# Key features from stacked high and low halves of a head, with scatters and evictions moved, in a graph and attention kernel on one Trainium2 core

## The chip, the cores and the metric

The kernel runs on one core of one Trainium2 chip. The metric is the device time of one execution in microseconds (us), taken as the median of several runs. TensorE, VectorE (DVE), ScalarE (ACT), GpSimd (POOL) and SyncE (SP) each run their own list of instructions and meet at semaphores.

## What is computed

The reference is a network of two layers over 1024 nodes of 512 features, with 16384 weighted edges. Most of it is untouched by the change: a graph product by segment sums, a mixture of eight experts, a second graph layer, a linear attention and a small table of integer steps. The change is in the block with kernelized attention, which runs twice (DEPTH = 2) with 8 heads of 64 and 256 features a head:

```python
def softmax_kernel(data, proj, is_query, eps=0.0001):
    normalizer = d ** (-0.25)
    ratio = proj.shape[0] ** (-0.5)
    data_dash = jnp.einsum('bhnd,md->bhnm', data * normalizer, proj)
    diag = jnp.sum(data ** 2, axis=-1, keepdims=True) * 0.5 * normalizer ** 2
    if is_query:
        m = jnp.max(data_dash, axis=-1, keepdims=True)
    else:
        m = jnp.max(data_dash, axis=(-2, -1), keepdims=True)
    return ratio * (jnp.exp(data_dash - diag - m) + eps)

for i in range(DEPTH):
    y = layernorm(x, ln1_g[i], ln1_b[i])
    # q, k, v: y @ W + b, cut into 8 heads
    qp = softmax_kernel(q, proj[i], True)
    kp = softmax_kernel(k, proj[i], False)
    d_inv = 1.0 / jnp.einsum('bhnm,bhm->bhn', qp, kp.sum(axis=2))
    ctx = jnp.einsum('bhnm,bhnd->bhmd', kp, v)
    o = jnp.einsum('bhmd,bhnm,bhn->bhnd', ctx, qp, d_inv)
    x = x + o @ Wo[i] + bo[i]
    y = layernorm(x, ln2_g[i], ln2_b[i])
    x = x + gelu(y @ W1[i] + b1[i]) @ W2[i] + b2[i]
```

The tables of the second graph layer (edge weights and edge counts, 1024 x 1024 each) are built meanwhile, by adding the edges one column of 128 at a time into two tables in memory.

## The kernel before

**Jobs and banks.** All work of TensorE is cut into jobs, each of which fills one of the eight PSUM banks in turn. `job_plan` (line 100) lists the stages in their order with the engines that empty a bank: "A" is ScalarE, "D" VectorE, "AD" both. Job n uses bank n mod 8, and `open_job` (L633) lets TensorE start it only when job n-8 has been emptied. Each engine's own loop is written out in the same order, so what stands late in one engine's list is late for all jobs behind it.

**Weights.** Every 512 x 512 block of weights is loaded into one of two `raw` buffers and split into a high half by ScalarE (`split_hi`, L1201) and a low half by GpSimd (`lo`, L2272), both float32r, in one of three slots of `W`. A product with it takes three single-pass products of 512 columns: high by high, high by low, low by high (L649 to L651, `split_mm`). `slot_order` says which block follows which in the slots; `w_wait` lets TensorE wait for the low half.

**A layer.** Queries and keys come out transposed, 128 rows (two heads) by 512 nodes a job: `q_T` and `k_T`, float32, written by ScalarE with the bias. VectorE writes the values `V` and their sum (L1710 to L1718). While the keys are made, VectorE also prepares edges for the scatters (`edge_batch`, L1641 to L1662: six batches in layer 0) and adds the bias `bo` to `X` (L1700). Then four head pairs follow. In each, TensorE computes

- `kd`: eight tiles of key features, one float32 product of 512 columns each, `k_T` by the two heads' `proj` (L804),
- `qd`: the same for queries, eight tiles, in the midst of which `kt` (L810, the transposed maxima of the keys) and `kb` (L815) stand,
- `ctx` (L831), the transposes `eT` of the query exponentials (L822) and the output `o` (L845).

VectorE takes the maxima of each key tile (L1732), their maximum over the tiles (`kmaxp`, L1738), the query maxima (L1742), evicts the transposed exponentials (`E_T`, L1759), and for each output takes a reciprocal (`rden`, L1776) and a product (`o_mul`, L1779); the low halves of the output (`op_a`, L1725) come a pair later. ScalarE copies the features and takes the exponentials. After the pairs come `wo`, `up` and `down` in four blocks each (`wo0`, `up0.0`, `down0.0` and so on; the last number is the block).

**GpSimd.** It makes the low halves and, between them, issues the scatters (`scatter`, L2334): for each column of 128 edges one indirect DMA into `table_w` and one into `table_c` (L2348), each of which waits for the last one into the same table. There are 128 pairs. How many stand between which low halves is written out in the loop.

```python
for name in ("wq", "wk", "wv"):
    if name != "wq":
        lo(f"{name}{l}")
    if l:
        scatter({"wq": 4, "wk": 6, "wv": 13}[name])
for hp, name in enumerate((f"wo{l}", f"up{l}.0")):
    if l == 0:
        scatter(10)
        pool.wait_ge(kdiag_ready, hp + 1)
    lo(name)
    if l:
        scatter(12)
scatter(12 if l else 4)
lo(f"down{l}.0")
```

## Time and profile before

| | |
|---|---|
| median of 3 runs | 1808.42 us (1804.3 to 1811.17) |
| the profiled execution, its time | 1808.56 us |
| its span | 1806.5 us |
| TensorE busy | 1676.0 us, 93% |
| VectorE busy | 1064.4 us, 59% |
| ScalarE busy | 695.4 us, 38% |
| GpSimd busy | 992.6 us, 55% |
| granted TensorE clock, mean | 0.97 of full speed |

The profile is one execution on the chip. A row of a timeline gives the start, the duration, the engine, the line of the kernel, the operation with the tiles that it writes and reads, their shapes, the number of instructions that were put into the row, and in brackets the idle time just before them with what ended it. A granted clock of 1.00 is 2.4 GHz, 0.50 is 1.2 GHz. Times in rows count from the start of the span. A float32 matmul leaves two records.

### The profile page before, as it was taken

How to read it: one execution, taken by the hardware profiler on the slowest of the kernel's cores; microseconds unless marked ns; L12 is line 12 of the kernel's file. 1: busy time of each engine (PE TensorE's matmuls, PEld its weight loads, DVE VectorE, ACT ScalarE, POOL GpSimd, SP SyncE). 2: the span in 40 equal slices, each digit the busy share in tenths (PEclk: the TensorE clock that was granted, in tenths of full speed). 3: DMA queues.
4: the chain of work that ended last, by engine and by line, in shares of the span. 5: the costliest groups of instructions: out<-in, count | busy, mean ns of one | idle time of the engine just before them, and what ended most of it. 6: DMA issues, size and time to landing. Idle time of an engine off the chain costs nothing.

```text
span 1806.5 us, 19998 instructions
## 1 busy us (share of the span) xinstructions
PE 1676.0 (93%) x7799; PEld 1302.2 (72%) x7799; DVE 1064.4 (59%) x1809; ACT 695.4 (38%) x916; POOL 992.6 (55%) x534
## 2 busy tenths in 40 slices
PE   6999999999989999999996999999999489999986
PEld 6766568788765457788875878777878478887863
DVE  7677878999936877543266442333333475432385
ACT  4535345333533443333412555556565221211112
POOL 4348412467777878588623666766676452333312
PEclk9999999999989999999996999999999799999998
DMA  9652102545422222322334878777775601121001
GB/s 342 172 161 24 24 1 73 128 120 108 103 27 24 1 24 1 93 48 47 99 129 168 292 249 272 247 262 246 269 248 180 198 8 57 60 70 55 16 0 47
DMA packets 146509, 212.05 MB, mean 117 GB/s; under 512 B 43724, under 2 KB 60336, under 8 KB 145168
## 3 DMA queue, kind: packets, MB, share of 16 engines
q1 hardware_dynamic: 98464, 176.96, 29.9%
q0 software_dynamic: 42832, 18.84, 8.5%
q10 hardware_dynamic: 5120, 14.99, 2.5%
q8 instruction: 62, 1.02, 0.2%
q14 instruction: 31, 0.25, 0.0%
HBM read 186.69 MB, written 30.08 MB: 120 GB/s over the span
## 4 chain that ended last, share of the span: by engine, by line
PE 73%; DVE 14%; POOL 4%; ACT 3%; issue 3%; DMA 3%; DVEq 0%; POOLq 0%
PE PS L649 19%; PE PS L651 18%; PE PS L650 18%; PE PS L804 5%; PE PS L831 3%; PE PS L845 3%; PE PS L822 2%; POOL table_c L2348 1%; POOL table_w L2348 1%; PE PS L692 1%; PE PS L986 1%; DVE h_op L1994 1%; DMA hg_dram<-hg 1%; DVE kmax L1732 1%; DVE picked L1648 1%
## 5 line engine op out<-in xcount | busy, mean ns | idle before, releaser
L2272 POOL TENSOR_TENSOR W<-raw,W 128x2048 fp32r<-128x2048 f32 x40 | 193.3, 4834 | 306.6 <-ACT W L1201 306.6
L2348 POOL DMA_INDIRECT table_w<-edge_add,edge_ix x128 | 204.2, 1595 | 109.2 <-DMA table_w<-edge_add,edge_ix 75.9
L2348 POOL DMA_INDIRECT table_c<-edge_add,edge_ix x128 | 206.4, 1613 | 59.5 <-issue 35.4
L649 PE MATMUL PS<-op_b,W 128*128 128x512 f32 x576 | 227.0, 394 | 6.6 <-DVE op_b L1628 3.3
L650 PE MATMUL PS<-op_b,W 128*128 128x512 f32 x576 | 225.4, 391 | 0.0
L651 PE MATMUL PS<-op_b,W 128*128 128x512 f32 x576 | 225.4, 391 | 0.0
L649 PE MATMUL PS<-W,op_a 128*128 128x512 f32 x480 | 187.8, 391 | 5.1 <-DVE op_a L1800 1.8
L651 PE MATMUL PS<-W,op_a 128*128 128x512 f32 x480 | 186.9, 389 | 0.0
L650 PE MATMUL PS<-W,op_a 128*128 128x512 f32 x480 | 186.8, 389 | 0.0
L2391 POOL TENSOR_TENSOR W<-raw,W 128x2048 fp32r<-128x2048 f32 x30 | 143.4, 4791 | 44.9 <-ACT W L1436 44.9
L1201 ACT ACTIVATE W<-raw 128x2048 fp32r<-128x2048 f32 x40 | 76.6, 1922 | 163.1 <-PE PS L651 104.9
L649 PEld LDWEIGHTS PS<-op_b,W 128*128 128x128 f32 x576 | 108.9, 189 | 32.0 <-DVE op_b L1628 3.8
L651 PEld LDWEIGHTS PS<-op_b,W 128*128 128x128 f32 x576 | 108.8, 189 | 23.0
L650 PEld LDWEIGHTS PS<-op_b,W 128*128 128x128 f32 x576 | 109.0, 189 | 22.3
L1370 ACT ACTIVATE G<-PS,colv 128x512 f32<-128x512 f32 x64 | 44.2, 691 | 179.6 <-PE PS L651 178.1
L649 PEld LDWEIGHTS PS<-W,op_a 128*128 128x128 f32 x480 | 90.1, 188 | 25.7 <-issue 3.2
L649 PE MATMUL PS<-W,x_op 128*128 128x512 f32 x248 | 98.7, 398 | 6.3 <-DVE x_op L1984 4.8
L651 PEld LDWEIGHTS PS<-W,op_a 128*128 128x128 f32 x480 | 90.1, 188 | 18.9
L650 PEld LDWEIGHTS PS<-W,op_a 128*128 128x128 f32 x480 | 90.1, 188 | 18.4
L1984 DVE TENSOR_TENSOR x_op<-PS,x_op 128x512 fp32r<-128x512 f32 x21 | 13.9, 688 | 145.6 <-ACT x_op L1443 145.6
L1800 DVE TENSOR_TENSOR op_a<-G,op_a 128x512 fp32r<-128x512 f32 x64 | 63.5, 1014 | 58.9 <-ACT op_a L1371 58.6
L1436 ACT ACTIVATE W<-raw 128x2048 fp32r<-128x2048 f32 x46 | 88.0, 1914 | 24.8 <-DMA raw<-in_L_ffn_w_dram 15.2
(426 smaller groups left out, 3774.7 us busy)
## 6 DMA issues: line engine op xcount, KB each, us to landing
raw<-in_L_ffn_w_dram SPq DMA_DIRECT2D x46, 1024.0 KB, 6.0
...
```

What stands on the lines that cost most here:

```text
L649: pe.matmul(ps, lhs_hi, rhs_hi, start=start, stop=False)
L650: pe.matmul(ps, lhs_hi, rhs_lo, start=False, stop=False)
L651: return pe.matmul(ps, lhs_lo, rhs_hi, start=False, stop=stop)
L804: pe.matmul(bank(n), feat[:, hp, t * P:(t + 1) * P], proj[:, :, :].rearrange("p a m -> p (a m)"), start=True, stop=True).then_inc(job_full, 1)
L831: mm = pe.matmul(bank(n)[:, (2 * h + mh) * VW:(2 * h + mh + 1) * VW], kd[:, h, t, mh * P:(mh + 1) * P], V[:, t, 2 * hp + h, :], start=(t = ...
L845: mm = pe.matmul(bank(n)[h * DH:(h + 1) * DH, :], ctx_sb[:, part, 2 * h + mh, :], E_T[:, 2 * h + mh, c * HALF:(c + 1) * HALF], start=(mh = ...
L1201: act.activation(W[:, s % SLOTS, 0, :], raw[:, raw_no[name] % 2, :], ACT.Copy).then_inc(hi_done, 1)
L1436: act.activation(ring_w[b % RING][:, 0, :], ring_raw[b % RING], ACT.Copy).then_inc(block_hi, 1)
L1800: dve.tensor_tensor(op_a[:, 1, at], G[:, j, :], op_a[:, 0, at].bitcast(F32), ALU.subtract).then_inc(hidden, 1)
L2272: pool.tensor_tensor(lo_at, raw[:, r % 2, :], hi_at.bitcast(F32), ALU.subtract).then_inc(lo_done, 1)
L2348: pool.indirect_dma_start(out=tb, out_offset=bass.IndirectOffsetOnAxis(ap=edge_ix[:, i, c:c + 1].bitcast(U32), axis=0), in_=edge_add[:, i, ...
L2391: pool.tensor_tensor(ring_w[b % RING][:, 1, :], ring_raw[b % RING], ring_w[b % RING][:, 0, :].bitcast(F32), ALU.subtract)\
```

## The change

**Keys.** `k_T` is replaced by two float32r stacks. `k_A` holds, in partitions 0 to 63, the high half of a pair's first head, and in 64 to 127 its low half; `k_B` holds the second head's low half in 0 to 63 and its high half in 64 to 127. ScalarE writes the high halves (two activations of 64 partitions in place of one of 128), VectorE the low halves (`key_lo`: two operations a key job, each reading PSUM and the high half in 64 partitions and writing the other 64). `proj_k` holds the projection's high and low half for both heads. A key tile becomes four float32r products of 256 columns: for each head, its stack by `proj_k`'s high and by its low half.

**Order.** The projection's transposes move from the end of the stage before into the key stage, behind key job 4. The last two edge batches move between the key jobs' low halves, and the `bo` additions behind them. The odd `E_T` evictions go to ScalarE. `k_B` lies in slot 1 of `W` and `rden` in slot 0, so `up{l}.0` takes slot 1 ahead of `wo{l}`'s slot 2, its high half is made after the last pair's query exponentials, and its low half after `wo`'s and all scatters up to there. GpSimd's scatters around `wv1`, `wo1` and `up1.0` are dealt out anew; their number stays.

```diff
@@ -102,19 +102,20 @@
...
     stages = [("xn_T", 4, "AD"), ("gnn_w_T", 4, "AD"), ("hg", 2, "A"), ("xn_T", 4, "AD"), ("par_T", 1, "D"), ("hg", 4, "A"),
-              ("y_T0", 4, "AD"), ("hg", 2, "A"), ("y_T0", 4, "AD"), ("edge_T", 1, "D"), ("proj0", 1, "A")]
+              ("y_T0", 4, "AD"), ("hg", 2, "A"), ("y_T0", 4, "AD"), ("edge_T", 1, "D")]
     for l in range(DEPTH):
...
             stages.append((f"q{l}", 8, "A"))
-        stages += [(f"k{l}", 1, "A"), (f"rq{l}", 2, "A"), (f"k{l}", 2, "A"), (f"dq{l}", 1, "A"), (f"k{l}", 5, "A"),
+        stages += [(f"k{l}", 1, "AD"), (f"rq{l}", 2, "A"), (f"k{l}", 2, "AD"), (f"dq{l}", 1, "A"), (f"k{l}", 2, "AD"),
+                   (f"proj{l}", 1, "AD"), (f"k{l}", 3, "AD"),
                    (f"v{l}", 1, "D"), (f"rk{l}", 2, "A"), (f"v{l}", 1, "D"), (f"dk{l}", 1, "A"), (f"v{l}", 6, "D"), (f"vsum{l}", 1, "A")]
...
             stages += [("kd" + s, 8, "AD"), ("qd" + s, 2, "A"), ("kt" + s, 1, "D"), ("qd" + s, 2, "A"),
-                       ("kb" + s, 1, "D"), ("qd" + s, 4, "A"), ("ctx" + s, 1, "D"), ("eT" + s, 8, "D"),
-                       ("o" + s, 4, "D")]
+                       ("kb" + s, 1, "D"), ("qd" + s, 4, "A"), ("ctx" + s, 1, "D")]
+            stages += [("eT" + s, 1, "A" if t % 2 else "D") for t in range(NT)] + [("o" + s, 4, "D")]
         stages += [(f"wo{l}", 6, "D"), (f"y2_T{l}", 4, "AD"), (f"wo{l}", 2, "D"),
@@ -122,7 +123,7 @@
...
             else:
-                stages += [(f"proj{l + 1}", 1, "A"), (f"down{l}.{fb}", 6, "D"), (f"y_T{l + 1}", 4, "AD"), (f"down{l}.{fb}", 2, "D")]
+                stages += [(f"down{l}.{fb}", 6, "D"), (f"y_T{l + 1}", 4, "AD"), (f"down{l}.{fb}", 2, "D")]
     stages += [("gnn", 6, "D"), ("xt_T", 4, "AD"), ("gnn", 2, "D"), ("gate_T", 1, "A"), ("xt_T", 4, "AD"), ("gate_T", 1, "A"), ("gate", 1, "D"),
@@ -229,8 +230,8 @@
...
     for l in range(DEPTH):
-        slot_order += [f"wq{l}", f"wk{l}", f"wv{l}", f"wo{l}"]
-        for fb in range(MLP):
+        slot_order += [f"wq{l}", f"wk{l}", f"wv{l}", f"up{l}.0", f"wo{l}", f"down{l}.0"]
+        for fb in range(1, MLP):
             slot_order += [f"up{l}.{fb}", f"down{l}.{fb}"]
@@ -280,7 +281,7 @@
...
         q_T = place("q_T", [P, NK, N], F32, at_a)
-        k_T = place("k_T", [P, NK, N], F32, at_a + 4 * 4096)
+        k_A = place("k_A", [P, NK, N], F32R, at_a + 4 * 4096)
         x_pair = place("x_pair", [P, NT, 2, D], F32R, at_b)
@@ -292,6 +293,7 @@
...
         W = place("W", [P, SLOTS, 2, BLK], F32R, at_w)
+        k_B = place("k_B", [P, NK, N], F32R, at_w + 4 * 2 * BLK)
         hg = place("hg", [P, NT, D], F32, at_w + 4 * 2 * 2 * BLK)
@@ -302,7 +304,8 @@
...
         o_mul = place("o_mul", [P, 2, HALF], F32, at_e)
-        rden = place("rden", [P, 2, HALF], F32, at_e + 4096)
+        rden = place("rden", [P, 2, HALF], F32, at_w)
+        proj_k = place("proj_k", [P, 2, NBF], F32R, at_e + 6144)
         tmp = place("tmp", [P, 4, D], F32, at_e)
@@ -768,7 +771,6 @@
...
 
-            projection_job(0)
             for l in range(DEPTH):
@@ -783,6 +785,8 @@
...
                             head_columns("q", l)
+                        if i == 1 and j == 4:
+                            projection_job(l)
                 w_wait(f"wv{l}")
@@ -797,12 +801,22 @@
...
                     s = f"{l}.{hp}"
-                    for x, feat in (("kd", k_T), ("qd", q_T)):
+                    if hp == 0:
+                        evacuated(f"proj{l}", 1)
+                        evacuated(f"k{l}", 8)
+                    for x in ("kd", "qd"):
                         for t in range(NT):
...
                             open_job(n)
-                            pe.matmul(bank(n), feat[:, hp, t * P:(t + 1) * P], proj[:, :, :].rearrange("p a m -> p (a m)"),
-                                      start=True, stop=True).then_inc(job_full, 1)
+                            mine = slice(t * P, (t + 1) * P)
+                            if x == "kd":
+                                for h, stack in enumerate((k_A, k_B)):
+                                    for i in range(2):
+                                        mm = pe.matmul(bank(n)[:, h * NBF:(h + 1) * NBF], stack[:, hp, mine], proj_k[:, i, :],
+                                                       start=(i == 0), stop=(i == 1))
+                            else:
+                                mm = pe.matmul(bank(n), q_T[:, hp, mine], proj[:, :, :].rearrange("p a m -> p (a m)"), start=True, stop=True)
+                            mm.then_inc(job_full, 1)
                             if x == "qd" and t == 1:
@@ -836,6 +850,7 @@
...
                     for c in range(2):
+                        evacuated("eT" + s, 4 * c + 3)
                         evacuated("eT" + s, 4 * c + 4)
@@ -862,8 +877,6 @@
...
                         feature_job(JOB_AT[f"up{l}.{fb}", j], op_b, slot_of[f"up{l}.{fb}"] % SLOTS, j % 4, j // 4)
-                    if fb + 1 == MLP and l + 1 < DEPTH:
-                        projection_job(l + 1)
                     w_wait(f"down{l}.{fb}")
@@ -1253,7 +1266,8 @@
...
                 act.activation(proj[0:DH, 0, :], bank(n)[0:DH, 0:NBF], ACT.Copy, scale=NORMALIZER)
-                act.activation(proj[DH:P, 1, :], bank(n)[DH:P, 0:NBF], ACT.Copy, scale=NORMALIZER).then_inc(job_act, 1)
+                act.activation(proj[DH:P, 1, :], bank(n)[DH:P, 0:NBF], ACT.Copy, scale=NORMALIZER)
+                act.activation(proj_k[:, 0, :], bank(n)[:, 0:NBF], ACT.Copy, scale=NORMALIZER).then_inc(job_act, 1)
 
@@ -1273,7 +1287,6 @@
...
             hi_half("y_T0", op_b, 1, ln_gb(0, 0), True)
-            projection_out(0)
             split_hi("wk0")
@@ -1291,22 +1304,29 @@
...
             for l in range(DEPTH):
-                for i, (x, dst) in enumerate((("q", q_T), ("k", k_T))):
+                for i, x in enumerate(("q", "k")):
                     for j in range(8):
...
                         m, c = j % 4, j // 4
+                        b = 8 + 4 * i + m
+                        cols = slice(c * HALF, (c + 1) * HALF)
                         if i == 0 and l and j == 2:
...
                             act.wait_ge(job_full, JOB_AT[f"rq{l}", j // 4] + 1)
-                        act.activation(G[:, j, :], bank(n), ACT.Square, bias=colv[:, l, 8 + 4 * i + m:9 + 4 * i + m]).then_inc(squared, 1)
-                        act.activation(dst[:, m, c * HALF:(c + 1) * HALF], bank(n), ACT.Identity,
-                                       bias=colv[:, l, 8 + 4 * i + m:9 + 4 * i + m]).then_inc(job_act, 1)
+                        act.activation(G[:, j, :], bank(n), ACT.Square, bias=colv[:, l, b:b + 1]).then_inc(squared, 1)
+                        if i == 0:
+                            act.activation(q_T[:, m, cols], bank(n), ACT.Identity, bias=colv[:, l, b:b + 1]).then_inc(job_act, 1)
+                        else:
+                            act.activation(k_A[0:DH, m, cols], bank(n)[0:DH, :], ACT.Identity, bias=colv[0:DH, l, b:b + 1])
+                            act.activation(k_B[DH:P, m, cols], bank(n)[DH:P, :], ACT.Identity, bias=colv[DH:P, l, b:b + 1]).then_inc(job_act, 1)
                         if i == 1 and j == 0:
...
                             columns_out("q", 0, l)
+                        if i == 1 and j == 4:
+                            projection_out(l)
                         if i == 0 and l and j == 2:
@@ -1314,7 +1334,6 @@
...
                 split_hi(f"wo{l}")
-                split_hi(f"up{l}.0")
                 if l == 0:
@@ -1354,6 +1373,13 @@
...
                         query_exp(t)
+                    if hp == HEADS // 2 - 1:
+                        split_hi(f"up{l}.0")
+                    for t in range(1, NT, 2):
+                        n = JOB_AT["eT" + s, t]
+                        act.wait_ge(job_full, n + 1)
+                        act.activation(E_T[:, :, t * P:(t + 1) * P], bank(n).rearrange("p (q n) -> p q n", q=4), ACT.Identity,
+                                       bias=eps_ones[:, 0:1]).then_inc(job_act, 1)
                 o_to_hi(HEADS // 2 - 1)
@@ -1375,7 +1401,6 @@
...
                     split_hi(f"wq{l + 1}")
-                    projection_out(l + 1)
                     for i in range(3):
@@ -1693,8 +1718,30 @@
...
                     dve.wait_ge(job_done, DONES[n])
-                for b in range(EARLY_BATCHES) if l == 0 else range(LATE_BATCH, EC // EB):
+                def key_lo(j):
+
+                    n = JOB_AT[f"k{l}", j]
+                    m, cols = j % 4, slice(j // 4 * HALF, (j // 4 + 1) * HALF)
+                    dve.wait_ge(job_act, ACTS[n])
+                    dve.scalar_tensor_tensor(out=k_A[DH:P, m, cols], in0=bank(n)[0:DH, :], scalar=colv[0:DH, l, 12 + m:13 + m],
+                                             in1=k_A[0:DH, m, cols].bitcast(F32), op0=ALU.add, op1=ALU.subtract)
+                    dve.scalar_tensor_tensor(out=k_B[0:DH, m, cols], in0=bank(n)[DH:P, :], scalar=colv[DH:P, l, 12 + m:13 + m],
+                                             in1=k_B[DH:P, m, cols].bitcast(F32), op0=ALU.add, op1=ALU.subtract).then_inc(job_done, 1)
+
+                first, past = (0, EARLY_BATCHES) if l == 0 else (LATE_BATCH, EC // EB)
+                for b in range(first, past - 2):
                     edge_batch(b)
+                for j in range(8):
+                    key_lo(j)
+                    if j == 1:
+                        edge_batch(past - 2)
+                    elif j == 3:
+                        edge_batch(past - 1)
+                    elif j == 4:
+                        n = JOB[f"proj{l}"]
+                        dve.wait_ge(job_act, ACTS[n])
+                        dve.scalar_tensor_tensor(out=proj_k[:, 1, :], in0=bank(n)[:, 0:NBF], scalar=NORMALIZER,
+                                                 in1=proj_k[:, 0, :].bitcast(F32), op0=ALU.mult, op1=ALU.subtract).then_inc(job_done, 1)
                 row_wait(f"bo{l}")
@@ -1768,7 +1815,7 @@
...
                     ins.then_inc(job_done, 1)
-                    for t in range(NT):
+                    for t in range(0, NT, 2):
                         e_t(t)
@@ -2354,15 +2401,13 @@
...
                     if l:
-                        scatter({"wq": 4, "wk": 6, "wv": 13}[name])
-                for hp, name in enumerate((f"wo{l}", f"up{l}.0")):
-                    if l == 0:
-                        scatter(10)
-                        pool.wait_ge(kdiag_ready, hp + 1)
-                    lo(name)
-                    if l:
-                        scatter(12)
-                scatter(12 if l else 4)
+                        scatter({"wq": 4, "wk": 2, "wv": 17}[name])
+                if l == 0:
+                    scatter(10)
+                    pool.wait_ge(kdiag_ready, 1)
+                lo(f"wo{l}")
+                scatter(36 if l else 14)
+                lo(f"up{l}.0")
                 lo(f"down{l}.0")
```

VectorE in the key stage of layer 0, before: behind the last edge batch (`edge_ix`) come the `bo` additions to `X` and then the values.

```order
L1652 TENSOR_REDUCE edge_add<-picked 128x2x4
L1656 TENSOR_SCALAR batch<-edge_add 128x8
L1658 SCALAR_TENSOR_TENSOR batch<-keycols,trash,batch 128x8 x2
L1662 TENSOR_SCALAR edge_ix<-batch,trash 128x8 x2
L1700 TENSOR_TENSOR X<-X,rowv 128x512 x8
L1710 COPY V<-dexp 128x64
L1711 TENSOR_TENSOR G<-PS,rowv 128x512
```

The same place in the changed kernel, from the end of the last batch: four more pairs of low halves of keys (four pairs stand ahead, around the batches) and the projection's low half.

```order
L1687 TENSOR_SCALAR edge_ix<-batch,trash 128x8 x2
L1726 SCALAR_TENSOR_TENSOR k_A<-PS,colv,k_A 64x512
L1728 SCALAR_TENSOR_TENSOR k_B<-PS,colv,k_B 64x512
L1743 SCALAR_TENSOR_TENSOR proj_k<-PS,proj_k 128x256
L1726 SCALAR_TENSOR_TENSOR k_A<-PS,colv,k_A 64x512
L1728 SCALAR_TENSOR_TENSOR k_B<-PS,colv,k_B 64x512
...
L1747 TENSOR_TENSOR X<-X,rowv 128x512 x8
L1757 COPY V<-dexp 128x64
```

The values now stand behind seventeen operations that were not there; the last edge batch stands ahead of the low halves of key jobs 4 to 7.

GpSimd in layer 1, before: the low half of `wk1`, then six pairs of scatters, then the low half of `wv1`.

```order
L2272 TENSOR_TENSOR W<-raw,W 128x2048
L2348 DMA table_w<-edge_add,edge_ix 1048704x1
L2348 DMA table_c<-edge_add,edge_ix 1048704x1
...
L2348 DMA table_w<-edge_add,edge_ix 1048704x1
L2348 DMA table_c<-edge_add,edge_ix 1048704x1
L2272 TENSOR_TENSOR W<-raw,W 128x2048
```

The same place in the changed kernel.

```order
L2319 TENSOR_TENSOR W<-raw,W 128x2048
L2395 DMA table_w<-edge_add,edge_ix 1048704x1
L2395 DMA table_c<-edge_add,edge_ix 1048704x1
L2395 DMA table_w<-edge_add,edge_ix 1048704x1
L2395 DMA table_c<-edge_add,edge_ix 1048704x1
L2319 TENSOR_TENSOR W<-raw,W 128x2048
```

Four pairs have moved behind the low half of `wv1`. Between the low half of `wo1` and the low halves of `up1.0` and `down1.0`, which now follow one another, stand 36 pairs; before, 12 stood between `wo1` and `up1.0` and 24 between `up1.0` and `down1.0`. In all, 55 pairs lie between the low halves of `wk1` and `down1.0` in both.

## Rows read from the trace of the kernel before

**Rows 1.** The page's first part: busy time, share of the span and instructions of each engine.

```profile
PE 1676.0 (93%) x7799; PEld 1302.2 (72%) x7799; DVE 1064.4 (59%) x1809; ACT 695.4 (38%) x916; POOL 992.6 (55%) x534
```

**Rows 2.** Waits of TensorE: engine line waited for, us in total, times, longest.

```profile
PE PS L810 <- DVE kmaxp L1738: 9.9, 6, 4.5
PE PS L649 <- POOL W L2272: 9.2, 2, 8.5
```

**Rows 3.** Timeline of TensorE, first head pair of layer 0: start, us, operation.

```profile
124.62 1.12 PE L797 MATMUL PS<-v_sum,eps_ones 128*128 128x512 f32 x2 [2.11 <-DVE V L1718]
...
134.32 0.27 PE L810 MATMUL PS<-ident,kmaxp 128*2 128x128 f32 x1
```

**Rows 4.** Timeline of TensorE, start of up1.0, its wait, and start of down1.0.

```profile
717.27 0.39 PE L649 MATMUL PS<-op_b,W 128*128 128x512 f32 x1
717.50 0.39 PE L650 MATMUL PS<-op_b,W 128*128 128x512 f32 x1
...
733.43 0.50 PE L649 MATMUL PS<-op_b,W 128*128 128x512 f32 x1 [3.35 <-DVE op_b L1628]
...
746.07 0.39 PE L649 MATMUL PS<-W,op_a 128*128 128x512 f32 x1
```

**Rows 5.** Timeline of TensorE, second head pair of layer 0.

```profile
157.87 7.13 PE L804 MATMUL PS<-proj,k_T 128*128 128x512 f32 x16
...
167.79 0.27 PE L810 MATMUL PS<-ident,kmaxp 128*2 128x128 f32 x1 [1.07 <-DVE kmaxp L1738]
```

**Rows 6.** Timeline of VectorE in the same stretch.

```profile
153.05 3.35 DVE L1776 RECIPROCAL rden<-PS 128x512 f32<-128x512 f32 x1
...
161.17 5.20 DVE L1732 TENSOR_REDUCE kmax<-PS 128x2 f32<-128x512 f32 x8
166.28 1.28 DVE L1725 TENSOR_TENSOR op_a<-o_mul,op_a 128x512 fp32r<-128x512 f32 x2
```

**Rows 7.** Windows: busy PE, PEld, DVE, ACT, POOL, then PEclk, DMA share, GB/s.

```profile
634.00:638.00 4.00, 4.00 (x7) 1.44 (x6) 2.84 (x9) 1.64 (x4) 1.93 (x2) 0.50 0.82 253
734.00:737.00 3.00, 3.00 (x8) 2.32 (x8) 3.00 (x4) 0.00 (x0) 0.00 (x0) 0.50 0.28 109
122.00:126.00 4.00, 1.89 (x6) 0.76 (x5) 1.99 (x3) 0.22 (x1) 0.00 (x0) 1.00 0.61 197
```

**Rows 8.** Timeline of VectorE, key and value stage of layer 0.

```profile
89.20 0.35 DVE L1646 SCALAR_TENSOR_TENSOR picked<-key_row,keycols,w_row 128x128 f32<-128x128 f32 x1 [0.85 <-DMA w_row<-in_edge_weight_dram]
...
97.03 4.99 DVE L1700 TENSOR_TENSOR X<-X,rowv 128x512 f32<-128x512 f32 x8
106.41 0.23 DVE L1710 COPY V<-dexp 128x64 f32<-128x64 f32 x1 [4.39 <-issue]
...
122.54 0.69 DVE L1711 TENSOR_TENSOR G<-PS,rowv 128x512 f32<-128x512 f32 x1 [0.57 <-PE PS L651]
123.27 0.69 DVE L1713 TENSOR_TENSOR v_sum<-v_sum,G 128x512 f32<-128x512 f32 x1
123.88 0.68 DVE L1718 TENSOR_TENSOR V<-G,dexp 128x512 f32<-128x512 f32 x1
```

**Rows 9.** Timeline of GpSimd: down0.0's low half; wk1's; scatters; down1.0's.

```profile
265.70 4.60 POOL L2272 TENSOR_TENSOR W<-raw,W 128x2048 fp32r<-128x2048 f32 x1 [58.21 <-ACT W L1201]
...
482.10 5.17 POOL L2272 TENSOR_TENSOR W<-raw,W 128x2048 fp32r<-128x2048 f32 x1
487.44 1.67 POOL L2348 DMA_INDIRECT table_w<-edge_add,edge_ix  x1 [0.17 <-issue]
...
491.31 1.55 POOL L2348 DMA_INDIRECT table_w<-edge_add,edge_ix  x1 [0.32 <-DMA table_w<-edge_add,edge_ix]
...
724.96 5.20 POOL L2272 TENSOR_TENSOR W<-raw,W 128x2048 fp32r<-128x2048 f32 x1
```

**Rows 10.** Timeline of TensorE: start of up0.0; first product of wv1.

```profile
282.84 0.39 PE L649 MATMUL PS<-op_b,W 128*128 128x512 f32 x1
...
521.82 0.80 PE L649 MATMUL PS<-W,op_b 128*128 128x512 f32 x1 [8.47 <-POOL W L2272]
```

## The prediction

> **What bounds the kernel now.** I read the page of the profile, the table of waits, the timelines of TensorE, VectorE and GpSimd, and windows with the granted clock. The page gives TensorE 93% of the span [rows 1], so the end is set by TensorE work plus what TensorE waits for. The table of its waits [rows 2] puts two of them in the part that the change touches: on the key maxima (9.9 us in six waits, the longest 4.5) and on GpSimd's low half of a weight block (8.5 us once). The timelines add 2.1 us on VectorE's values before the value sum [rows 3] and 3.35 us on VectorE's `op_b` [rows 4]. They also show the order inside a head pair. From the start of the key products to the `kt` transpose TensorE needs 157.87 to 167.79 [rows 5]; meanwhile VectorE does two reciprocals with their multiplies (from 153.05 to 161.17), eight key maxima to 166.28, and two low halves of the output [rows 6]. TensorE waits only 1.07 us there, so in the three later pairs of a layer VectorE is already the longer of the two. In the first pair it is TensorE: from the value sum at 124.62 to `kt` at 134.32 [rows 3] VectorE only follows tile by tile.
>
> **Key products.** A key tile is now one float32 product of 512 columns in two records, 16 records in 7.13 us with the last one's tail of some 0.25, or 0.86 us a tile [rows 5]. It becomes four float32r products of 256 columns. A float32r product of 512 columns starts 0.23 us after the one before [rows 4], of which 0.213 is its columns at 2.4 GHz. Half the columns and the same rest give 0.12 us, a tile 0.48. No row has 256 float32r columns; the bounds are 0.11 us (columns alone) and 0.23, and I take 0.12, by its own columns.
> First pair of a layer: the maxima, eight in 5.20 us or 0.64 each [rows 6], become the bound. `kt` comes 9.7 us after the value sum (124.62) in before [rows 3]; the first maximum moves 0.4 us forward and eight take 5.1 instead of 6.7, so 2.0 us are gained.
> Later pairs: VectorE's chain stands. Four of its eight `E_T` evictions go to ScalarE, which idles there, but the first reciprocal then waits for its own product instead, 0.2 us sooner. TensorE has keys and two query tiles done 5.6 us after the start of the pair (the last two key tiles wait for banks that the second reciprocal and multiply free) and waits for `kt` until 9.7 us: a gap of 4.0 us in place of 1.07.
>
> **What a gap costs.** Just behind the gaps of 4.5 us (ending near 634) and 3.35 us (ending at 733.43) the granted clock is 0.50, that is 1.2 GHz [rows 2, 4, 7]; around the 2.1 us wait of layer 0 it is 1.00 [rows 7]. After the 3.35 us gap 48 products take 12.64 us instead of 10.9 [rows 4]: 1.7 us lost. I take a fall in each 4.0 us gap at 1.7 us; bounds are 0 (as after 2.1 us) and 2.3, half of a low stretch that covers 634 to 638. Net of the 0.2: +1.5 us a pair, +4.5 for three pairs of layer 0.
>
> **Low halves of the keys, layer 0.** VectorE gets sixteen operations of 64x512 and one of 128x256. Eight `X` adds of 512 columns take 4.99 us, 0.62 each, overlapped; Among V's operations one that waits for the last one's result starts 0.73 us after it (122.54, 123.27), one that doesn't 0.61 (123.27, 123.88) [rows 8]. Columns set the time, so half the partitions save nothing. I take 0.67, the middle of the two: 10.7 us, and 0.35 for the projection (half the columns): 11.1. From the end of the fourth edge batch (88.35: the next row at 89.20 less its 0.85 us of idle) VectorE has the last two batches (89.20 to 97.03 = 7.8) and the adds (5.0). With 11.1 more it starts on V at 112.3 instead of 106.41. V's eight tiles need three operations each, two for the first: 15.8 us; they had 18.15 (106.41 to 124.56). So of 5.9 us, 2.35 are absorbed: V ends 3.5 us later. TensorE's wait for it grows from 2.1 to about 4.4 us (it ends a little later itself, since the projection's transposes wait 1.2 us for a bank that the first key's low half frees), and the clock falls: +1.3 us, the rest hidden under the maxima. The projection's transposes only move. ScalarE's third activation per key tile fits: three at its mean of 0.76 us (695.4 / 916 [rows 1]) against 2.7 us of TensorE (12 x 0.227). Layer 0: 3.5 + 1.3 - 2.0 + 4.5 = **+7.3 us**.
>
> By the Trainium skill, "VectorE: DVE Perf Modes", section "Two Vector instructions with no wait between them", an instruction that starts in another 32-partition group than the last one is held until all earlier ones are finished. Nothing here shows it for before. By it, each half, alternating between partitions 0 and 64, costs its full length. That is the second rival.
>
> **GpSimd, layer 1.** A scatter is a pair of issues; two pairs start 3.87 us apart here [rows 9] (table_w at 487.44, then 491.31), and 55 of them, counted in the kernel, lie between the low halves of wk1 (ending 487.27) and down1.0 (starting 724.96), with three 5.2 us subtractions among them. The change puts 2 instead of 6 ahead of wv1. Even at 5 us a pair that low half ends near 487.3 + 10 + 5.2 = 502.5, before TensorE asks at 521.82 - 8.47 = 513.35 [rows 10]: the 8.5 us wait goes, and about 1.9 of cold clock with it. But up1.0's low half now stands behind all 55 scatters, since its slot holds `k_B`. Against down1.0's start in before, one subtraction and the transfer stall behind it (2.1, an estimate) drop out: it starts at 717.6 and ends at 722.8. TensorE began up1.0 at 717.27 [rows 4]. Without this wait it would now come near 705: -8.5 and -1.9 at wv1, -2.0 in the first pair, -3.5 and -1.1 for the 4.5 us wait, whose subtraction moves away, +4.5 for gaps. So it waits some 18 us, and all that layer 1 gains is lost in this wait. What counts is up1.0's start, +5.6 us, and the cold clock behind the wait, +1.8. Then down1.0's subtraction runs just behind up1.0's and no longer blocks `op_b`: -3.35 and -1.7 [rows 4]. Layer 1: **+2.3 us**.
> VectorE's later keys cost nothing in layer 1: V starts about 1 us late with 2.35 to spare, and the wait at up1.0 covers it. Layer 0 has no such wait: GpSimd idles 58.21 us before a subtraction at 265.70 [rows 9], and up0.0 is wanted at 282.84 [rows 10]. GpSimd's stream before layer 1 hangs on ScalarE's halves in the MLP, so it moves with TensorE by layer 0's +7.3.
>
> **Sum.** 1808.56 (profiled execution; the median of the runs is 1808.42, so no correction) + 7.3 + 2.3 = **1818.2 us**. About 0.5% is what a measurement tells from no change, 9.0 us; the sum lies just beyond.
>
> **Rivals.**
> *The clock stays up in the three gaps of layer 0.* A few late matmuls in the gap may be enough, as at 2.1 us. For: the gap starts with single tiles that wait for banks. Against: 3.3 us had its fall. It decides if the gap's idle part stays under about 2.5 us, between the two. Price -5.1: 1813.1, not slower by my bound. Chance 0.17.
> *Each low half of a key runs unoverlapped.* 0.67 becomes 0.77 (0.73 from the dependent rows [rows 8], 0.04 as an allowance for the scalar operand): 16 x 0.10 = 1.6 us more, all of it on V's end: 1819.8. For: halves alternate their partitions. Against: no row. Chance 0.20. The Trainium skill's page named above says it would be so.
> *up1.0's low half is in time.* Then layer 1 gives -12.5 and -5.1 instead of +2.3: 7.3 - 17.6 = -10.3, 1798.3. The scatters would have to run at 3.4 us or less; the issue itself is 1.55 to 1.67 us twice [rows 9]. Chance 0.04.
> *The 256-column products are not single-pass.* At four passes a tile takes 1.7 us: `kt` 8.9 us later than forecast in the first pair and 4.1 in each later one (no gap, so no fall), about +22 in all: 1840. Float32r rows at 512 columns speak against it. Chance 0.04.
> *The rest*, 0.10: scatter waits for transfers shorter by a few us, or V less late: 1808 to 1815.
> The forecast itself has 0.45.
>
> **Numbers.** The bounds (clock 0 to 2.3 us a gap, low halves 0.62 to 0.77, the scatter stream by 3 us either way) spread the forecast by some 5 us each way, so 0.55 of it and 0.65 of the second rival lie over +9.0. Slower: 0.25 + 0.13 + 0.03 + 0.04 + 0.02 = 0.47. Faster: 0.05. The same: 0.48. Range 1806 to 1827: it leaves out the two far rivals and the tails.
>
> **What would show it.** TensorE's waits: kmaxp near 4 us six times; POOL W about 18 us once, before up1.0, at about 712 to 730; none before wv1. The value wait of layer 0 over 4 us. Key products near 0.48 us a tile, scatters unchanged. The clock at 0.50 behind each `kt` gap. I am wrong if up1.0 starts within a microsecond of its last wo product, or if layer 0's attention ends as early as before.

## The result and the profile after

The changed kernel takes 1835.87 us (median of 4 runs, 1834.65 to 1838.41) against 1807.26 us before: the ratio is 1.015, with a 95% interval of 1.0123 to 1.0177. It is slower by some 28 us, where 1818.2 with a range to 1827 was forecast. The profiled execution has a span of 1834.4 us against 1806.5. A few executions, of the kernel before and of the last experiment's (1823.69 us), fell into a slower state of the chip and are left out of every ratio here.

The page of the changed kernel, first part, answers to [rows 1]: TensorE does less work, 1673.4 us, and the span is longer.

```profile
PE 1673.4 (91%) x7927; PEld 1325.1 (72%) x7927; DVE 1078.6 (59%) x1811; ACT 725.3 (40%) x966; POOL 993.2 (54%) x534
```

The table of TensorE's waits in the changed kernel (columns as in [rows 2]):

```profile
PE PS L824 <- DVE kmaxp L1785: 22.8, 8, 3.6
PE PS L652 <- POOL W L2319: 14.3, 1, 14.3
...
PE PS L801 <- DVE V L1765: 6.9, 2, 4.7
PE PS L652 <- DVE op_a L1847: 6.0, 1, 6.0
...
PE PS L845 <- ACT kd L1373: 3.5, 1, 3.5
```

The first three were forecast, in kind and nearly in size. The last two were not: a wait for `op_a` in the MLP of layer 0, and one for the key exponentials. To see where the time went, I laid the starts of TensorE's stages side by side. The difference between the two kernels at each (after less before, us) is:

| TensorE starts | before | after | later by |
|---|---|---|---|
| value sum, layer 0 | 124.62 | 129.55 | 4.9 |
| `ctx` of pair 0 | 140.17 | 148.42 | 8.2 |
| transposes of pair 0 | 147.26 | 162.10 | 14.8 |
| output of pair 0 | 150.85 | 167.02 | 16.2 |
| output of pair 3 | 251.35 | 271.33 | 20.0 |
| up0.0 | 282.84 | 302.62 | 19.8 |
| up0.1 | 330.25 | 356.93 | 26.7 |
| queries of layer 1 | 462.86 | 497.06 | 34.2 |
| values of layer 1 | 521.82 | 546.60 | 24.8 |
| wo1 | 693.64 | 709.62 | 16.0 |
| up1.0 | 717.27 | 747.68 | 30.4 |
| down1.0 | 746.07 | 773.31 | 27.2 |
| up1.1 | 767.83 | 795.07 | 27.2 |

So layer 0 loses 20 us up to its MLP, of which 11 in the first head pair alone; then 7 and 7.5; layer 1 gains 18 up to `wo1`, and gives 14 of it back at `up1.0`.

**The first pair.** TensorE in the changed kernel, from `ctx` of pair 0 to the `kt` transpose of pair 1:

```profile
148.42 13.89 PE L845 MATMUL PS<-V,kd 128*128 128x65 f32 x64 [3.52 <-ACT kd L1373]
162.10 4.99 PE L836 MATMUL PS<-ident,G 128*128 128x128 f32 x32
...
183.42 0.37 PE L824 MATMUL PS<-ident,kmaxp 128*2 128x128 f32 x1 [3.57 <-DVE kmaxp L1785]
```

`ctx` waits for the key exponentials and then takes 13.89 us for 64 products that take 7.25 in the later pairs. The window of this stretch (columns as in [rows 7]) has the clock at 1.2 GHz throughout:

```profile
148.00:164.00 16.00, 15.58 (x73) 15.61 (x74) 2.89 (x9) 6.54 (x14) 11.76 (x8) 0.50 0.30 47
```

Why are the exponentials late? VectorE there, and GpSimd:

```profile
140.17 0.16 DVE L1791 TENSOR_TENSOR nqmax<-nqmax,dexp 128x2 f32<-128x2 f32 x1
...
141.40 3.98 DVE L1791 TENSOR_TENSOR nqmax<-nqmax,dexp 128x2 f32<-128x2 f32 x1
...
146.09 0.15 DVE L1801 COPY nkmax<-PS 128x2 f32<-128x2 f32 x1
```

```profile
140.86 4.50 POOL L2319 TENSOR_TENSOR W<-raw,W 128x2048 fp32r<-128x2048 f32 x1 [0.29 <-DVE kdiag L1797]
```

An addition of two columns takes 3.98 us instead of 0.16, and ends as GpSimd's subtraction for `wo0` ends (140.86 + 4.50 = 145.36). `nkmax`, for which ScalarE waits, stands behind it. In the kernel before, the same subtraction began 4.6 us after the copy of `nkmax`:

```profile
137.71 0.15 DVE L1754 COPY nkmax<-PS 128x2 f32<-128x2 f32 x1
```

```profile
142.32 5.09 POOL L2272 TENSOR_TENSOR W<-raw,W 128x2048 fp32r<-128x2048 f32 x1
```

The change moved VectorE's work in this pair 4.6 us later (its maximum `kmaxp` from 134.00 to 138.57) and the subtraction 1.5 us sooner (142.32 to 140.86), 6.0 in all: more than the margin.

### The profile page after: what moved, and what is told of

Same layout as the page of the kernel before. It is cut to its first block, busy times and chain, and to the rows that moved or that the text cites. A ratio compares the mean times of both kernels' runs of the same rounds, so it can differ in the third digit from the quotient of the medians.

```text
span 1834.4 us, 20315 instructions
## 1 busy us (share of the span) xinstructions
PE 1673.4 (91%) x7927; PEld 1325.1 (72%) x7927; DVE 1078.6 (59%) x1811; ACT 725.3 (40%) x966; POOL 993.2 (54%) x534
## 4 chain that ended last, share of the span: by engine, by line
PE 62%; DVE 16%; POOL 10%; DMA 5%; issue 4%; ACT 2%; SPq 0%; DVEq 0%; POOLq 0%; ACTq 0%
PE PS L652 18%; PE PS L654 18%; PE PS L653 18%; POOL table_w L2395 4%; POOL table_c L2395 4%; PE PS L845 2%; DMA table_c<-edge_add,edge_ix 1%; PE PS L818 1%; DMA key_dram<-edge_f 1%; PE PS L695 1%; DVE rden L1823 1%; DMA table_w<-edge_add,edge_ix 1%; POOL slots_x L2431 1%; POOL W L2319 1%; DVE kmax L1779 1%
## 5 line engine op out<-in xcount | busy, mean ns | idle before, releaser
L652 PE MATMUL PS<-op_b,W 128*128 128x512 f32 x576 | 226.5, 393 | 16.8 <-POOL W L2319 14.3
L2031 DVE TENSOR_TENSOR x_op<-PS,x_op 128x512 fp32r<-128x512 f32 x21 | 13.9, 688 | 146.2 <-ACT x_op L1468 146.2
```

The costliest lines, as they stand in the source:

```text
L652: pe.matmul(ps, lhs_hi, rhs_hi, start=start, stop=False)
```

## The experiments

I call the reading above theory 1: a GpSimd subtraction holds up a VectorE operation with two inputs in SBUF, and the loss is made of separate waits, each at its place. Every kernel was timed beside the kernel before on the same chip; what is compared is the ratio to it (the changed kernel's is 1.015).

### wo0's low half two scatters later

```diff
                     pool.wait_ge(kdiag_ready, 1)
+                    scatter(2)
                 lo(f"wo{l}")
-                scatter(36 if l else 14)
+                scatter(36 if l else 12)
```

> The changed kernel, with two of GpSimd's scatters moved ahead of the low half of wo0, so that it starts some 7 us later, when the query maxima of the first pair are done. Theory 1 (GpSimd's subtraction at 140.86 held VectorE's 128x2 addition of the query maxima for 3.98 us, so the key exponentials and ctx were late): the addition takes 0.16 us again, the 3.52 us wait before ctx and the long stretch at 1.2 GHz behind it go, 11 us less, near 1825. Rival (the low clock of the first pair comes from the longer wait for the values before it, and would be there anyway): the wait before ctx goes, but ctx still takes near 13.9 us, some 4 us less, near 1832.

1821.96 us, ratio 1.0071 (1.0053 to 1.0089): 14 us less. The subtraction now runs from 148.74, every addition takes 0.16 us, and:

```profile
145.86 7.25 PE L845 MATMUL PS<-V,kd 128*128 128x65 f32 x64
```

The wait is gone, and so is the low clock; the rival, by which `ctx` would have stayed at 13.9 us, falls. The transposes of pair 0 begin at 152.95, 5.7 us after those of before instead of 14.8. A second wait went with it, the 5.08 us ahead of layer 1, to which I come below.

### The same collision made in the kernel before

```diff
-                        scatter(10)
+                        scatter((8, 12)[hp])
```

> The kernel before, with two of the ten scatters ahead of the low half of wo0 moved behind it, so that it starts as soon as the key maximum of the first pair is known, near 136. Theory 1 (the subtraction there holds VectorE's additions, whatever the keys' products are): an addition of 4 us near 136.8, ctx some 3.5 us late, and the clock falls in ctx: 8 to 12 us more, 1815 to 1819. Rival (the loss of the changed kernel in that pair belongs to its later values and its own keys): no change, within 2 us of 1807.

1826.79 us, ratio 1.01 (1.0082 to 1.0118). Nothing of the keys was touched here. VectorE, GpSimd and TensorE of this kernel:

```profile
137.41 3.97 DVE L1744 TENSOR_TENSOR nqmax<-nqmax,dexp 128x2 f32<-128x2 f32 x1
```

```profile
136.87 4.50 POOL L2272 TENSOR_TENSOR W<-raw,W 128x2048 fp32r<-128x2048 f32 x1 [1.41 <-DVE kdiag L1750]
```

```profile
144.43 13.89 PE L831 MATMUL PS<-V,kd 128*128 128x65 f32 x64 [3.52 <-ACT kd L1354]
```

The same 3.5 us wait and the same 13.89 us as in the changed kernel: the pair's output starts 12.4 us late, 0.6 of them from ahead of the value sum, as theory 1 has it. The time grew by more than forecast (18 us). The shift brought a second collision further on: the transposes ahead of layer 1 wait 4.53 us, and layer 1's queries start 20.7 us late. Some of that comes back at wv1, where TensorE waits 3.59 us instead of 8.47.

All sixteen traces agree on this place. In eight of them a held addition (3.97 to 5.46 us) stands ahead of the copy of `nkmax`, and from `ctx` to the transposes are 13.2 to 13.7 us; in the other eight none does, and it is 7.1 us.

### The high half of up0.1 behind the last GELU

In the changed order of slots `up0.1` takes the slot of `up0.0`. ScalarE's high half of it stands behind the fourth GELU and must wait until `up0.0` has done its last product; the other four GELUs stand behind it. ScalarE in the changed kernel, and TensorE in the second half of `down0.0`:

```profile
326.34 1.92 ACT L1214 ACTIVATE W<-raw 128x2048 fp32r<-128x2048 f32 x1 [9.61 <-PE PS L654]
```

```profile
343.15 0.80 PE L652 MATMUL PS<-W,op_a 128*128 128x512 f32 x1 [5.96 <-DVE op_a L1847]
```

```diff
-                        if j == 3 and fb + 1 < MLP:
+                        if j == (7 if fb == 0 else 3) and fb + 1 < MLP:
                             split_hi(f"up{l}.{fb + 1}")
```

> The changed kernel, with ScalarE's high half of up0.1 and up1.1 moved behind the last GELU of up0.0 and up1.0 (in the changed kernel it stands behind the fourth GELU and waits 9.6 us for its slot, which up0.0 holds until its last product). Theory 1 (that wait makes the GELUs of jobs 4 to 7 late, and with them the second half of down0.0): the 5.96 us gap in down0.0 goes, 6 to 7 us less, near 1829. Rival (the gap comes from GpSimd's two subtractions that hold VectorE's multiplications, which still stand there): the gap stays over 3 us, less than 3 us gained, 1833 or more.

1826.08 us, ratio 1.0094 (1.0074 to 1.0113): 10 us less. The wait is gone (up0.1 starts 18.0 us after that of before, not 26.7), so the gap does not come without ScalarE's wait. The 5.08 us wait ahead of layer 1 went with it, as in the first experiment.

This leaves open what the subtractions do. In the changed kernel two of them (at 328.34 and at 334.76) run while VectorE works on the block's `op_a` and an edge batch. VectorE and GpSimd there:

```profile
329.44 4.66 DVE L1847 TENSOR_TENSOR op_a<-G,op_a 128x512 fp32r<-128x512 f32 x2 [4.78 <-ACT op_a L1397]
...
334.82 4.64 DVE L1673 SCALAR_TENSOR_TENSOR picked<-key_row,keycols,order 128x128 f32<-128x128 f32 x1
...
341.80 1.29 DVE L1847 TENSOR_TENSOR op_a<-G,op_a 128x512 fp32r<-128x512 f32 x2
```

```profile
328.34 4.61 POOL L2319 TENSOR_TENSOR W<-raw,W 128x2048 fp32r<-128x2048 f32 x1 [36.06 <-ACT W L1214]
```

The two rows take 4.66 and 4.64 us where the same work takes 1.29 and 0.34 elsewhere, 7.7 us more, and the `op_a` at 341.80, for which TensorE waits from 337.19, stands behind both. In this experiment the subtractions still hold VectorE (`op_a` takes 5.71 us at 329.61), but no `op_a` of the block is left behind them. So ScalarE's wait pushed the low halves of `op_a` in among the two subtractions and an edge batch; by these rows the wait needs both. No run takes the subtractions away alone.

### The key products issued twice

```diff
-                                for h, stack in enumerate((k_A, k_B)):
+                                for h, stack in ((0, k_A), (1, k_B)) * (2 if hp else 1):
```

> The changed kernel, with the four products of each key tile issued twice in the pairs 1 to 3 of each layer (the second time overwrites the first with the same values). Theory 1 (VectorE bounds these pairs, and TensorE's 3.57 us wait for kmaxp costs only the clock that falls behind it): the wait shrinks to under 1 us, the clock stays at 1.00, a pair takes 33.4 us instead of 34.5, and layer 0 is 3 to 4 us shorter: near 1832. Rival (the products are on the path): 8 x 0.48 us more in each of three pairs of layer 0, 11 us more, near 1847.

1836.19 us, ratio 1.0153 (1.0126 to 1.0181): no change, which is between the two. The rows show why. In pairs 1 to 3 the wait for `kmaxp` falls from 3.57 us to

```profile
220.28 0.27 PE L824 MATMUL PS<-ident,kmaxp 128*2 128x128 f32 x1 [1.06 <-DVE kmaxp L1785]
```

and the clock behind it stays up: 1.00 in the window from 220 to 223, against 0.50 from 220 to 222 in the changed kernel. That gives back 1.5 us a pair (from `kt` to `ctx` 5.84 us instead of 7.37). But `kt` itself comes 17.7 us after the output's start instead of 16.4: VectorE, which never idles among its eight maxima in the changed kernel, waits 0.72 and 0.27 us there for key tiles (in the third pair). A pair has 34.3 us with the products doubled, 34.5 without, 33.5 before the change, so the 3 to 4 us that were forecast for layer 0 are 1.5. Twice the work on TensorE costs nothing: in these pairs the shorter products buy a longer wait.

### The output's low halves behind the query maxima

```diff
-                    if hp:
-                        for c in range(2):
-                            o_to_lo(hp - 1, c)
                     dve.wait_ge(job_done, DONES[JOB["kd" + s] + 7])
...
                             dve.tensor_copy(nkmax[:, :], bank(n)[:, 0:2]).then_inc(job_done, 1)
+                    if hp:
+                        for c in range(2):
+                            o_to_lo(hp - 1, c)
```

> The changed kernel, with VectorE's two low halves of the last pair's output (1.28 us in each later pair) moved from ahead of the key maximum to behind the last query maximum. Theory 1 (TensorE waits 3.57 us for VectorE's chain, and the clock falls for it): the wait becomes 2.3 us, each pair is 1.3 us shorter, and up to 1.4 more where the clock then stays up; three pairs of layer 0 count, those of layer 1 only shorten the way to the wait at up1.0: 4 to 8 us less, 1828 to 1832. Rival (the later pairs are bound elsewhere): no change, within 2 us of 1836.

1828.3 us, ratio 1.0105 (1.0083 to 1.0128): 7.6 us less, so VectorE's chain is what TensorE waits for in these pairs. Each wait is 2.49 us instead of 3.57. Behind the 3.57 us waits of the changed kernel the clock fell six times in six; behind those of 2.49 us three times in six here; behind those of 1.06 us never. Over the five kernels below and here that have this edit and the new keys, it fell behind 19 of 30 waits of 2.5 us, so at this length the fall is not settled by the length alone.

### Eight pairs of scatters behind down1.0's low half

```diff
-                scatter(36 if l else 14)
+                scatter(28 if l else 14)
                 lo(f"up{l}.0")
                 lo(f"down{l}.0")
+                if l:
+                    scatter(8)
```

> The changed kernel, with 8 of the 36 pairs of scatters of layer 1 moved from ahead of the low half of up1.0 to behind that of down1.0. Theory 1 (the stream of scatters alone holds up1.0 back, 14.26 us in the changed kernel): 8 pairs at 3.73 us are 30 us, the wait before up1.0 goes with the low clock behind it, 14 to 17 us less, near 1820. Rival (something else would hold up1.0, its high half on ScalarE or VectorE's op_b): a wait stays there, less than 7 us gained, 1829 or more.

1822.03 us, ratio 1.0065 (1.0041 to 1.0089): 14 us less. GpSimd's two subtractions at the end of the wait in the changed kernel, and TensorE's first product behind them:

```profile
742.53 9.60 POOL L2319 TENSOR_TENSOR W<-raw,W 128x2048 fp32r<-128x2048 f32 x2
```

```profile
747.68 0.80 PE L652 MATMUL PS<-op_b,W 128*128 128x512 f32 x1 [14.26 <-POOL W L2319]
```

With eight pairs fewer ahead, the two subtractions run from 710.71, and up1.0 starts 21.6 us after that of before instead of 30.4. The 14.26 us wait is gone, but from wo1's start to up1.0's are still 29.9 us, 6 more than in the kernel before (23.6): the subtractions now meet VectorE's low half of the output:

```profile
713.65 7.38 DVE L1772 TENSOR_TENSOR op_a<-o_mul,op_a 128x512 fp32r<-128x512 f32 x1 [0.70 <-ACT op_a L1351]
```

### The low half of wq1 one scatter later

VectorE's eight additions of a bias to `X` at the end of layer 0 take 10.38 us in the changed kernel, with GpSimd's subtraction for `wq1` at 471.86 among them; before, it began at 446.38, just behind the last of them (441.17 + 4.94 = 446.11). TensorE's transposes of layer 1's first layer norm wait 5.08 us for what follows.

```profile
467.84 10.38 DVE L1860 TENSOR_TENSOR X<-X,rowv 128x512 f32<-128x512 f32 x8
```

```profile
471.86 5.21 POOL L2319 TENSOR_TENSOR W<-raw,W 128x2048 fp32r<-128x2048 f32 x1
```

```diff
-                        scatter(4 if l else (0, 3, 3, 3, 3, 3, 4, 3)[2 * fb + i])
+                        scatter(4 if l else (0, 3, 3, 3, 3, 3, 5, 2)[2 * fb + i])
```

> The changed kernel, with one pair of scatters moved from behind to ahead of the low half of wq1, which then starts 3.7 us later, when VectorE's eight additions to X at 467.84 are done. Theory 1 (the subtraction holds them for 5.4 us and TensorE waits 5.08 us for the layer norm behind them, but up1.0 is set by GpSimd's stream, which this does not shorten): the additions take 4.9 us, the wait and its low clock go and layer 1 starts 6 to 7.5 us sooner, the wait before up1.0 grows by as much, and the time stays within 3 us of 1836. Rival (every wait of TensorE in the chain counts): 6 to 7.5 us less, near 1829.

1839.2 us, ratio 1.0161 (1.0136 to 1.0186): no gain. The additions take 4.95 us, layer 1's queries start 5.5 us sooner than in the changed kernel, and the wait before up1.0 is 18.4 us instead of 14.3. This is the loss of the table (7.5 us before layer 1) that costs nothing here: GpSimd's stream sets up1.0, and does not care when TensorE comes. In the eight kernels that have the new keys and 36 pairs of scatters there, it needs 268.0 to 271.0 us from the low half of wq1 to that of up1.0.

### VectorE's bias additions in the third head pair

```diff
-                row_wait(f"bo{l}")
-                for t in range(NT):
-                    ins = dve.tensor_tensor(X[:, t, :], X[:, t, :], rowv[:, row_at[f"bo{l}"] % 3, :], ALU.add)
-                link(ins)
                 row_wait(f"bv{l}")
...
+                    if hp == 2:
+                        row_wait(f"bo{l}")
+                        for t in range(NT):
+                            ins = dve.tensor_tensor(X[:, t, :], X[:, t, :], rowv[:, row_at[f"bo{l}"] % 3, :], ALU.add)
+                        link(ins)
+
                     def e_t(t):
```

> The changed kernel, with VectorE's eight additions of the output bias to X (4.9 us) moved from ahead of the values to the third head pair, behind its query maxima, where VectorE idles for 6 us. Theory 1 (in layer 0 the seventeen new operations and these make the values late): TensorE's wait for the values goes from 4.75 to 2.1 us, the value sum comes 2.6 us sooner, and the key maximum then comes before GpSimd's subtraction, so that the 3.98 us addition and the fall of the clock in ctx may go too: 3 to 14 us less, 1822 to 1833. Rival (the values are late because TensorE's key stage is longer): the value sum stays where it is, within 2 us of 1836.

1819.32 us, ratio 1.0052 (1.0032 to 1.0073): 17 us less, more than forecast. TensorE's wait for the values is 2.11 us again, the value sum starts at 128.47, and with `kt` at 135.98 the copy of `nkmax` (139.37) comes ahead of the subtraction (141.72), which still holds an addition, now one for which nobody on the path waits:

```profile
139.37 0.15 DVE L1797 COPY nkmax<-PS 128x2 f32<-128x2 f32 x1
...
141.20 5.63 DVE L1787 TENSOR_TENSOR nqmax<-nqmax,dexp 128x2 f32<-128x2 f32 x1
```

So 3 us more or less on VectorE decide over 11: the collision is a matter of timing, and the new operations are all still there.

### Low halves of the keys in the order A, A, B, B

```diff
-                    key_lo(j)
+                    if j in (0, 2, 5):
+                        key_lo(j, (0,))
+                        key_lo(j + 1, (0,))
+                        key_lo(j, (1,))
+                        key_lo(j + 1, (1,))
+                    elif j in (4, 7):
+                        key_lo(j)
```

> The changed kernel, with the low halves of the key jobs 0 and 1, 2 and 3, 5 and 6 made in the order A, A, B, B instead of A, B, A, B, so that two operations in turn read and write the same partitions. Rival 2 of the prediction (an operation that begins in other partitions than the last is held until that one has ended): from A to A and from B to B 0.61 to 0.67 us, from A to B and on to the next A 0.76 to 0.79. Against it (these operations never overlap, whatever their partitions): 0.76 to 0.79 everywhere. In neither case over 0.7 us in all, which a time can't tell.

One execution, 1834.46 us; what counts is in the rows. (`key_lo` gets a second argument, which says whether it makes the A or the B half.) In the changed kernel each half costs 0.76 to 0.79 us from start to start:

```profile
87.62 0.74 DVE L1726 SCALAR_TENSOR_TENSOR k_A<-PS,colv,k_A 64x512 fp32r<-64x512 f32 x1
88.38 0.76 DVE L1728 SCALAR_TENSOR_TENSOR k_B<-PS,colv,k_B 64x512 fp32r<-64x512 f32 x1
89.17 0.74 DVE L1726 SCALAR_TENSOR_TENSOR k_A<-PS,colv,k_A 64x512 fp32r<-64x512 f32 x1
```

With two of a kind in turn (the same operation twice in one row):

```profile
88.42 1.40 DVE L1727 SCALAR_TENSOR_TENSOR k_A<-PS,colv,k_A 64x512 fp32r<-64x512 f32 x2
89.83 1.43 DVE L1730 SCALAR_TENSOR_TENSOR k_B<-PS,colv,k_B 64x512 fp32r<-64x512 f32 x2
```

Two of them end 1.40 us after the first began, one alone takes 0.74: they start 0.66 us apart, and A to B stays near 0.76. This is the prediction's second rival. By the Trainium skill, "VectorE: DVE Perf Modes", section "Two Vector instructions with no wait between them", a start in another 32-partition group is held until all earlier instructions have finished; these rows agree.

### The edits together

The first four edits (wo0's low half, up0.1's high half, the eight pairs, the output's low halves) in one kernel:

> The changed kernel with the four edits together: wo0's low half two scatters later, the high half of up0.1 and up1.1 behind the last GELU, 8 pairs of scatters of layer 1 behind down1.0's low half, and the output's low halves behind the query maxima. Theory 1 (four separate losses, each at its place): layer 0 ends 24 to 32 us sooner than in the changed kernel, layer 1 has no long wait before up1.0: 1780 to 1790, faster than both kernels. Rival (the waits replace one another, since VectorE, ScalarE and GpSimd are all near the path): over 1800.

1793.05 us, ratio 0.9917 (0.9899 to 0.9935): faster than both kernels, 43 us less than the changed one, where the four alone sum to 14 + 10 + 14 + 8 = 46. The rival (the waits replace one another, over 1800) falls. The time lies 3 us above the range of the forecast (1780 to 1790). The wait ahead of layer 1 (4.72 us) is there, and no long wait at up1.0 covers it, so it could be the reason. The next kernel tries that, with the later low half of wq1:

> The four edits together (1793.1 us) and wq1's low half one scatter later. Theory 1: TensorE no longer waits at up1.0 there, so the 4.72 us wait of the layer norm at 463.94 and its clock now count: 6 to 7.5 us less than 1793, near 1786. Rival (VectorE's additions collide with something else): within 2 us of 1793.

1795.31 us, ratio 0.9921 (0.9906 to 0.9936): no gain, where 6 to 7.5 us were forecast. Layer 1's queries start 7.3 us sooner, as expected, and `wo1` still 5.4 us sooner, but all of it is lost before up1.0, where the layer norm comes late. The rows of TensorE, VectorE and GpSimd:

```profile
700.68 1.54 PE L695 MATMUL PS<-ident,G 128*128 128x128 f32 x6 [6.33 <-DVE G L1639]
```

```profile
691.16 9.46 DVE L1639 TENSOR_SCALAR G<-X,mv,rstd 128x512 f32<-128x512 f32 x4
```

```profile
689.04 9.64 POOL L2319 TENSOR_TENSOR W<-raw,W 128x2048 fp32r<-128x2048 f32 x2
```

Four TENSOR_SCALAR operations take 9.46 us (2.24 in the kernel before, ahead of layer 1), while the two subtractions run until 698.68. With the bias additions moved as well:

> The same with VectorE's bias additions in the third head pair as well. Theory 1: the value sum of layer 0 comes 2.6 us sooner and the clock stays up there: 3 to 4 us less than the kernel with wq1's low half later, near 1782.5. Rival (the additions delay ctx_sb or meet a subtraction of GpSimd in layer 1): no gain, or a loss of up to 5 us.

1793.78 us, ratio 0.9904 (0.9888 to 0.9921), which overlaps with the last one's interval; 1782.5 was forecast. The value sum comes 4 us sooner, the wait before up1.0 stays (6.32 us), and one of 3.67 us ahead of layer 1 is new: there the subtraction for wq1 (448.74) now holds the layer norm's four TENSOR_SCALAR, which take 6.29 us. And with 12 instead of 8 pairs moved, to take the subtractions away from the layer norm:

> The kernel with all six edits (1793.8 us), with 12 instead of 8 pairs of scatters of layer 1 behind down1.0's low half. Theory 1 (the two subtractions, now at 689.0 to 698.7, hold VectorE's TENSOR_SCALAR of the layer norm before up1.0 for 9.46 us, and TensorE waits 6.33 us for it): the first subtraction runs near 674, the second near 684, the TENSOR_SCALAR takes 2.2 us again, 5 to 9 us less, 1785 to 1789. Rival (the layer norm is late for another reason, such as the bias additions or ScalarE's square root): the wait stays over 4 us, within 2 us of 1794.

1799.7 us, ratio 0.9945 (0.9923 to 0.9966): 6 us more, where 5 to 9 less were forecast. The TENSOR_SCALAR operations take 1.92 us again, which shows what held them; but the first subtraction now holds the output's low half (5.03 us at 670.96; `wo1` waits 4.87 us), and TensorE waits for a low half of GpSimd once more further on, behind the scatters that were moved. The second of these waits:

```profile
886.76 0.76 PE L652 MATMUL PS<-op_b,W 128*128 128x512 f32 x1 [7.21 <-POOL W L2321]
```

### Order alone, on the old keys

The kernel before, with the output's low halves moved as above, and:

```diff
-                        scatter({"wq": 4, "wk": 6, "wv": 13}[name])
+                        scatter({"wq": 4, "wk": 2, "wv": 17}[name])
...
-                scatter(12 if l else 4)
+                scatter(4)
                 lo(f"down{l}.0")
+                if l:
+                    scatter(8)
```

> The kernel before, with its keys as they are, and three edits of order alone: VectorE's output low halves behind the query maxima, 2 instead of 6 pairs of scatters ahead of wv1's low half (17 instead of 13 behind it), and 8 pairs moved behind down1.0's low half. Theory 1 (the single-pass keys give nothing that counts, and the gain of the best kernel comes from order): the 8.47 us wait at wv1 with its clock goes, six waits of 1.07 us go, and op_b is not held at 730: 15 to 22 us less, 1786 to 1793. Rival (the gain of the combined kernel needs the shorter key products): 1798 or more.

1799.0 us, ratio 0.9934 (0.9908 to 0.996). In its profiled execution the waits at wv1 and for `kmaxp` are gone, as theory 1 has it, but 5.69 and 4.76 us are lost at two other places. It settles little: 1799 is the rival's number, but its interval overlaps with those of the best kernels with the new keys (0.9917, 0.9904), and its runs spread from 1789 to 1800. So most of what the best kernels gain over before is order and needs no new keys; whether the shorter products add one or two tenths of a per cent stays open. The profiled executions point that way: the second four `xt_T` transposes, behind the whole part that is edited, begin at 936.17 here, at 933.66 and 931.27 in the kernels with four and six edits, and at 948.33 before. This kernel's profiled execution (1790.69 us) is short for its median because the part behind them, which no edit touches, took 852.5 us in it, against 856.0 to 861.6 in the other fifteen.

## Why the prediction was wrong

The direction was right, the size was not. By its own steps:

- **Later pairs**, forecast at +1.5 us each and 4.5 in layer 0: 3.8 us (from 16.2 to 20.0). The waits are 3.57 us where 4.0 was forecast, and the clock falls in each, so the rival "the clock stays up" fell. The key products take 0.48 us a tile, as taken; that the last two tiles wait for banks shows in no row, they follow at the same 0.48.
- **Low halves of the keys**, forecast at 0.67 us each and V 3.5 us late: 0.76 to 0.79 each, and the value sum 4.9 us late. A mis-sized term; the second rival had it.
- **"So 2.0 us are gained" in the first pair, and nothing changes behind `kt`.** This step failed, and it is the largest error: -2.0 and +1.3 for the clock were forecast, and 11.2 us are lost between the value sum and the output. The gain itself was sized well. From the value sum to `kt` are 9.70 us before and 7.51 where the clock stays up (bias additions later); in the changed kernel they are 9.34, with some three of the eight key tiles at 1.2 GHz behind the value wait (products 0.21 us apart instead of 0.12). The error is behind `kt`, where the prediction put GpSimd's subtraction for `wo0` at nothing: `ctx` comes 3.7 us later after it (9.53 instead of 5.85), and `ctx` and the transposes take 7.9 us more at the low clock. The rows of before had a margin of 4.6 us there, and the change used 6.0. The prediction knew the effect, since in layer 1 it counts as gains two waits of TensorE behind such subtractions (3.5 and 3.35 us) that go away. It did not look for new ones in layer 0.
- **"`up{l}.0` takes slot 1" was costed at nothing for the blocks behind it.** Slot 1 is then asked for by up0.1, whose high half stands in the midst of up0.0's GELUs: 5.96 us of wait and 6.9 in all, with two subtractions that hold VectorE in between. In layer 1 TensorE does not wait in that place; VectorE has no edge batches there, but whether that is why was not tried.
- **Layer 1**, forecast at +2.3 us against GpSimd's stream: GpSimd's low half of wq1 is 25.5 us late (471.86 against 446.38) and the program ends 27.9 us late, so +2.4. The mechanism was right: the wait of 8.47 us at wv1 goes, 14.26 us at up1.0 take its place (18 forecast), and what layer 0 loses up to wq1 is what the program loses. It is why the 7.5 us ahead of layer 1 don't count.

In numbers: 7.3 us were forecast for layer 0, and 25.5 measured where GpSimd's stream takes it over. Of the 18.2 between them the first pair makes 11.9 (11.2 instead of 1.3 - 2.0), up0.1's slot 6.9, the values 1.4, the later pairs -0.7; the last -1.4 are the way from the pairs to the MLP (-0.2) and GpSimd's stream, 1.2 less late than up0.1. Both large terms came from how the engines' lists met in time, none from the length of the new products. That each of the three large places is real (these two, and up1.0), the runs show: 14, 10 and 14 us came back by single edits. What put wq1's subtraction 1 us earlier against the additions is not separated from chance: it came and went between the kernels (4.53 to 5.08 us in eight of them, 3.67 in one, under 2 in seven).
